# Four graph layers in one program: in the second attention layer, one VectorE operation weights the values of a whole step

## What is computed

```
q = (xn @ Wq + bq).reshape(n, H, DH)          # n 3125, H 8, DH 32
k = (xn @ Wk + bk).reshape(n, H, DH)
v = (xn @ Wv + bv).reshape(n, H, DH)
ep = ef @ We + be
scores = einsum('ehd,ehd->eh', q[dst], k[src] + ep[:, None, :]) * scale
scores = scores * ew[:, None]
ex = exp(scores - segment_max(scores, dst)[dst])
out = segment_sum(ex[:, :, None] * v[src], dst) / segment_sum(ex, dst)
```

## Time and profile before

| | us |
|---|---|
| three runs | 7702.69, 7706.99, 7715.14 |
| median | 7706.99 |
| profiled execution | 7714.56 |
| its span, first to last instruction | 7712.8 |

### The profile page before, as it was taken

One profiled execution on the slowest core, in us unless ns is written; L12 is line 12 of the kernel. 1 busy time (PEld: TensorE's weight loads), 2 busy tenths in 40 slices (PEclk: granted clock), 3 DMA queues, 4 the chain that ended last, 5 costly groups with the idle time before them and its releaser, 6 DMA issues. The chain is left out here.

```text
span 7712.8 us, 119806 instructions
## 1 busy us (share of the span) xinstructions
PE 5533.7 (72%) x30906; PEld 4182.6 (54%) x30906; DVE 4805.5 (62%) x14770; ACT 3687.5 (48%) x11072; POOL 5209.9 (68%) x5181
## 2 busy tenths in 40 slices
PE   6777675555559898967888888797555555767774
PEld 5666665555546666644666666564443444545553
DVE  8666666666658788877999999311222224555555
ACT  1333333222247777754888888332000003777773
POOL 4777777777777777743777776212777773777773
PEclk9777787777789999988999999898777777888786
DMA  4333341111145665645777776313444444444443
GB/s 146 78 80 79 79 110 34 36 36 34 36 110 155 159 157 155 157 120 145 202 200 200 202 202 172 110 58 92 109 109 108 109 108 73 109 110 110 109 110 88
DMA packets 1041601, 885.39 MB, mean 115 GB/s; under 512 B 749049, under 2 KB 857617, under 8 KB 1040823
## 3 DMA queue, kind: packets, MB, share of 16 engines
q0 software_dynamic: 259600, 658.46, 31.6%
q1 hardware_dynamic: 726977, 162.08, 11.1%
q10 hardware_dynamic: 54374, 57.20, 2.2%
HBM read 736.38 MB, written 140.99 MB: 114 GB/s over the span
## 5 line engine op out<-in xcount | busy, mean ns | idle before, releaser
L1302 POOL DMA_INDIRECT edges_kv<-kv,edges_rec x1712 | 1867.5, 1091 | 569.2 <-issue 473.2
L1449 PE MATMUL banks<-edges_kv,edges_hot 128*128 128x288 f32 (+2 forms) x5136 | 1482.4, 437 | 310.4 <-DVE edges_kv L1777 232.5
L1449 PEld LDWEIGHTS banks<-edges_kv,edges_hot 128*128 128x128 f32 x5136 | 1024.4, 210 | 577.7 <-issue 324.7
L1968 POOL DMA_INDIRECT edges_rows<-rel,edges_rec x856 | 809.4, 946 | 382.1 <-issue 257.1
L574 POOL DMA_INDIRECT by_src_records<-sort_by_src_rec,sort_by_src_pos_i x808 | 798.4, 988 | 326.6 <-issue 225.1
L1302 POOL DMA_INDIRECT edges_kv<-feat,edges_rec x856 | 828.5, 968 | 268.6 <-issue 242.8
L1984 PE MATMUL banks<-edges_rows,edges_hot 128*128 128x256 f32 x1712 | 630.3, 533 | 462.5 <-DMA edges_rows<-rel,edges_rec 423.3
L574 POOL DMA_INDIRECT by_dst_records<-sort_by_dst_rec,sort_by_dst_pos_i x808 | 787.5, 975 | 246.4 <-issue 241.5
L661 DVE SCALAR_TENSOR_TENSOR sort_junk<-banks,sort_hot_lo 128x128 bf16<-128x128 f32 x1616 | 437.7, 287 | 659.7 <-PE banks L723 646.6
L1984 PEld LDWEIGHTS banks<-edges_rows,edges_hot 128*128 128x128 f32 x1712 | 434.2, 266 | 658.8 <-DMA edges_rows<-rel,edges_rec 263.8
L1604 ACT ACTIVATE edges_off<-columns,edges_column 128x128 bf16<-128x128 f32 x2568 | 785.7, 393 | 0.0
(11 more groups left out here) (456 smaller groups left out, 11919.1 us busy)
## 6 DMA issues: line engine op xcount, KB each, us to landing
edges_kv<-kv,edges_rec POOLq DMA_INDIRECT x1712
sort_feat<-in_edge_attr_dram SPq DMA_DIRECT2D x100, 256.0 KB
rel<-tables_stage SPq DMA_DIRECT2D x100, 252.0 KB
by_dst_records<-by_dst_blank ACTq DMA_DIRECT2D x21, 800.0 KB
edges_rec<-by_dst_records SPq DMA_DIRECT2D x26, 592.0 KB, 7.6
by_src_records<-by_src_blank ACTq DMA_DIRECT2D x1, 13696.0 KB, 52.1
edges_rows<-rel,edges_rec POOLq DMA_INDIRECT x856, 2.7
edges_kv<-feat,edges_rec POOLq DMA_INDIRECT x856
```

What stands on the lines that cost most here:

```text
L1302: pool.indirect_dma_start(kv[:, r, c, 0:koff + DIM], None, tab, bass.IndirectOffsetOnAxis(ap=reci[:, b, c, idx:idx + 1], axis=0)).then_inc ...
L1449: last = pe.matmul(ps[:, 6 + m % 2, 0:OW], hot[:, b % 2, c, :], kv[:, b % BUFS, c, koff:koff + OW], start=(c % 2 == 0), stop=(kind != 1 an ...
L1968: pool.indirect_dma_start(rows[:, r, c, :], None, tab, bass.IndirectOffsetOnAxis(ap=reci[:, b, c, idx:idx + 1], axis=0)).then_inc(gathered ...
```

## The change

In the second attention layer (`kind == 1`) `weigh` takes all eight tiles at once, at the place where it took half 0. The call for half 1 is left out, and PE waits for one count per step instead of two. The other layers are as they were.

```
-                    pe.wait_ge(msg_done, n(2, h + 1))
+                    pe.wait_ge(msg_done, n(1, 1) if kind == 1 else n(2, h + 1))
...
-                    t, r = slice(4 * h, 4 * h + 4), b % BUFS
+                    t, r = slice(0, G) if kind == 1 else slice(4 * h, 4 * h + 4), b % BUFS
...
-                    if oldest:
+                    if oldest and kind != 1:
                         weigh(*oldest, 1)
```

## The result

The changed kernel is slower: 7833.94 us (median of 4 runs, 7825.72 to 7836.95) against 7710.74 (4 runs, 7702.69 to 7715.14), a ratio of 1.0158 with a 95% interval of 1.0146 to 1.0170. The profiled execution has a span of 7824.0 us, 111.2 more than before. The second attention layer accounts for all of it: from the first L1804 to the end of the last it takes 1331.1 us instead of 1208.9, 122.2 more; the parts ahead of it and behind it are 4.8 and 6.2 us shorter. A step takes 12.52 us on average instead of 11.32.

A forecast was written before the change was run, and what follows sets the result against it. PE and ACT's ring was taken to set the 11.30 us step, with POOL's gathers taking over after the change: (12.6 - 11.3) x 102 = 133 us on 7707 gives 7840 us, range 7775 to 7895.

The forecast's parts named there:

- POOL binds: Second attention layer: held gathers make POOL set the step, 12.6 us instead of 11.3; chance 0.80.
- The floor of 12.1: POOL's least step: 10.0 us for eight gathers, plus 0.90 held by the weighting and 1.18 by L1804.
- The block of 2.28 us: Whole weighting L1777 on DVE, longer than the gather's 1.25 us cycle; holds one gather, ending 0.82 behind it.
- The second statement: Skill's rule, kept as rival: tensor_tensor doesn't stall GpSimd's DMA; change costs nil, 7707 us; no change had chance 0.10.
- The freed gather: Gather beginning 1.12 us behind the weighting, 0.10 after L1756, held until L1804 ends; costs 1.18 us a step.
- Steps of 12.1 to 13.15: Forecast range of the second attention layer's step, with 12.6 us taken amid three walked values.
- The walk: Gather starts followed through one closed step for three data delays, giving steps of 13.15, 12.78 and 12.28 us.
- L1817's waits go: Sign in the second attention layer: DVE's waits at L1817 for PE, 16.4 us in 1000, disappear.
- L1449 does not wait for the weighting: PE's L1449 starts on time, the weighting ending 0.05 us later; the rival, up to 7819 us, had chance 0.04.
- The margin of 0.3 us: Time left between the weighting's end on DVE and PE's start of L1449, so PE does not wait.
- The clock: A granted PE clock below 1.00 in the layer would be a further cost, not counted in the forecast.

The follow-up runs named there:

- psum_weights: Changed kernel with L1777's small operand read from PSUM bank 4 instead of SBUF, plus two waits: 7736.11 us, ratio 1.0023 to the kernel before.
- psum_bank_only: Changed kernel with exponentials moved to PSUM bank 4 and the same added waits, but weights still read from SBUF: 7854.76 us, ratio 1.0179 to the kernel before.
- halves_together: Changed kernel with the weighting as two operations of four tiles, back to back at the first half's place: 7716.59 us, ratio 0.9999 to the kernel before.
- gap_before_product: Changed kernel with one DVE wait ahead of the second half's L1804 until L1756 has finished: 7727.86 us, ratio 1.0005 to the kernel before.
- swap_last_two: Changed kernel with L1756 ahead of L1755 in all three attention layers: 7838.22 us, ratio 1.0157 to the kernel before.
- pads_before_product: Changed kernel with two more short operations like L1756, output unread, between L1755 and L1756: 7859.19 us, ratio 1.0198 to the kernel before.
- split_5_3: Changed kernel with the weighting as two operations of 5 and then 3 tiles at the same place: 7707.85 us, ratio 0.9999 to the kernel before.

## Why the prediction was right

**POOL binds.** Right, in kind and in size. Forecast 7840, measured 7834; forecast 133 us for 102 steps of 12.6, measured 122.2 for the layer and 12.52 for the step. The gathers' mean was forecast at 1.28 and came out at 1.256. The floor of 12.1 was made of two blocks, 0.90 and 1.18 us. They measured 1.00 behind the weighting and 0.98 behind the second L1804, a step; 0.43 more came behind the first L1804, which the floor left out. The 1.41 behind the two L1804 were 1.05 before; the 1.00 behind the weighting were 0.24.

**The block of 2.28 us always catches a gather.** Right: 103 of 107 steps, and the end 0.82 behind the weighting. psum_weights against psum_bank_only shows the cause, two SBUF operands. The second statement cited from the Trainium skill ("SBUF — State Buffer", section "Who interferes with whom"), that a tensor_tensor was not seen to stall a DMA that GpSimd issues, does not hold for these gathers: by it the two kernels would take the same time, and they are 119 us apart.

**The freed gather is caught a second time.** Right as an event: in 98 of 107 steps a gather ends 0.82 behind the second L1804, in 86 of them after more than 1.7 us. What the forecast did not say is that this block was there before as well (103 gathers of over 1.7 us; the 2.01 of the earlier trace rows is one). New is only that it now comes on top of the first. Both are needed: without the first (psum_weights, halves_together) or without the second (gap_before_product) next to no loss is left. The reason given, that L1756 catches the gather and hands it on, is not borne out. With an operation that reads PSUM ahead of L1804 the gather is held as well (swap_last_two), and under a chain of short operations on two SBUF operands it gets through at the first seam if L1804 had not been passed on (pads_before_product).

**Steps of 12.1 to 13.15, and DVE waits in every step.** The walk assumed a step closed on itself. There is none: steps run from 11.1 to 14.6 (5% and 95%), 30 of 106 are under 11.5, and the first L1804 waited over 0.1 us in 53. That 12.6, picked amid three walks of a step that does not occur, came within 0.1 of the mean is in part luck. The gathers get ahead in some steps and fall behind in others; the mean is POOL's. So L1804 waits 62.0 us in 1000, not over 100. DVE's busy time fell by 93 us in 1000 (971.55 to 878.68); 60 of these went into waits for gathers and 31 into waits of L1817 for PE.

**L1817's waits go, and L1449 does not wait for the weighting.** Both wrong, without effect on the time. L1817 waits 47.4 us instead of 16.4. The first L1449 starts 0.10 us behind the end of L1777, which is as soon as it can, in 51 of 107 steps (4 before). When DVE has stood for a gather, all that hangs on it is late, and PE then waits for DVE and DVE for PE's next product. The margin of 0.3 us holds only in steps in which DVE is on time; these waits follow from POOL's, as their going in gap_before_product shows (L1817 6.1 us; L1449 at once behind the weighting in 7 steps).

**The clock.** PE's granted clock fell from 1.00, the level of 2.4 GHz, to a mean of 0.94 in the same stretch, where PE now stands idle more (busy 825.69 us instead of 857.71); with the gap it is 0.99. The step follows from the gathers alone (12.45 of 12.52), so no cost of it can be seen.

## What to carry to other kernels

An engine that issues indirect gathers all the time is a clock of its own: add its instructions and pauses up before merging VectorE operations, because one operation on two SBUF operands that is longer than the gathers' cycle catches one nearly every time (103 of 107 steps here). What a merged operation saves at VectorE (0.07 us here) is small beside the 1.0 us of a held gather; cut it just behind the place where a gather starts, or bring one operand from PSUM. If two such operations lie close together, a wait of VectorE for itself between them, 0.1 us long, may be worth 1 us a step.

## What the runs showed that was not expected

- Whether a gather that starts 0.1 us behind a short operation is held by the long L1804 that follows goes with whether VectorE's sequencer had already passed L1804 on at that moment, and neither with the operand of the short operation nor with the offset of L1804: 433 held and 73 free gathers in five runs, parted without an exception within each run. A wait of 0.1 us ahead of L1804 freed all of them.
- The seam between two long operations of the same kind lets a gather go although they overlap by the same 0.07 us (split_5_3: 1.21 us instead of some 2.0), and a gather held by L1777 goes at its end although L1745, with one operand in PSUM, adjoins. Why these seams let it through and those ahead of an L1804 that has been passed on do not, no run here tells: length, number of partitions and form changed together.
- The order of two pieces, 5 and 3 tiles or 3 and 5, moved the whole program by 1.7%, through the phase in which a gather meets the seam.
